# The first two batches of a graph layer put in another order on every engine

## The chip, the cores and the metric

The kernel runs on one core of a Trainium2 chip. The metric is the device time of one execution in microseconds. The core has a matrix engine (TensorE, PE in the rows), VectorE (DVE), ScalarE (ACT), GpSimd (POOL) and SyncE (SP), which here only issues transfers; all five run their own instruction streams and meet at semaphores.

## What is computed

There are 16 graphs (batches) of 512 nodes with 128 features, and a 512x512 adjacency `adj` for each. In the reference both adjacencies `A1` and `A2` are `adj`.

```python
h = jnp.maximum(_layernorm(x, axis=-1), 0.0)
...
eye = jnp.zeros_like(A1) + jnp.eye(N, dtype=A1.dtype)
shifted = jnp.roll(eye, 1, axis=0)
A_fwd = [A1, A2, shifted]
A_list = A_fwd + [jnp.swapaxes(a, 1, 2) for a in A_fwd]
A_list.append(eye)
HW = jnp.einsum('bnf,rfo->rbno', features, W[:, :F]) + jnp.einsum('rd,rdo->ro', W_edges, W[:, F:])[:, None, None, :]
AHW = jnp.einsum('rbnm,rbmo->rbno', A, HW)
out = jnp.max(AHW, axis=0) + b
```

The result is `x + out`. There are seven relations: 0 and 1 with the adjacency, 3 and 4 with its transpose, 2, 5 and 6 with a permutation or identity. A maximum is taken over all seven. Everything is float32.

## The kernel before, in words

The kernel keeps nodes or features on the 128 partitions; `C` = 4 chunks of 128 nodes make a batch. Each float32 operand of a product is split into a rounded part and a rest (`a_hi`, `a_lo`; `at_hi`, `at_lo` for the transposed adjacency; `h_hi`, `h_lo`; `ht_hi`, `ht_lo`; `w_hi`, `w_lo`), and every product is three matmul passes (hi hi, lo hi, hi lo; L697 to L699, in `passes`). ScalarE makes the rounded parts, VectorE and GpSimd subtract to get the rests.

A batch `b = 2k + q` goes through these steps. `x` and four chunks of the adjacency arrive (`x_loaded`, `a_loaded`). VectorE takes mean and variance (`moments`, `mean_and_variance`), a reciprocal root and a shift follow, and ScalarE writes the normalised `h_sb`. TensorE transposes the adjacency (`turn_a`, four transposes for each of four rows of blocks), `h` (`turn_h`) and the row sums (`turn_sums`). Then come `bwd` (four groups of three passes, with `a_hi`, `a_lo`) and `fwd` (four groups, with `at_hi`, `at_lo`), `eye(r)` for relations 2, 5 and 6 (`EYE[0]`, `EYE[1]`, `EYE[2]`) and `along(r)` for the other four, which run one batch later. `join_first` on ScalarE writes `best`, and `join(r)` on VectorE takes the maximum with each further relation, in the order 2, 5, 6, 0, 1, 3, 4. `turn_best` turns the result back, `finish` adds `x` plus bias (`xb_sb`) into `o_sb`, and SyncE stores it.

The row sums take a way of their own: `take_sums` copies them out (`sum_rows`), SyncE writes them to memory and reads them back spread over all partitions (`spread_sums`), and `fill` scales them by `c_col` into the PSUM bank of a relation before `along` accumulates onto it. `c_col` itself, seven columns, comes once from a small matmul of `we_sb` and `wedge_cols`, which VectorE copies out.

Each engine's order is written out by hand: a start of its own for batch 0, `first_step()` (the rest of batch 0 with the beginning of batch 1), `later_batches` (which calls `step` for batch 1, loops over the middle ones and ends with batches 14 and 15), and a last part. The first batch is special: its row-chunks of `h` are rounded singly, and its PSUM banks are others (`rel_bank`, `at_bank`).

SyncE's queue is a single stream: `x` and adjacency of batch 0, `x` of batch 1, small tensors, adjacency of batch 1, `w_sb`, `bias_sb`. After that `reload_x` waits for `h_ready` and `xb_ready` of the buffer's last batch, and `spread_sums` stands behind `reload_a`.

## Time and profile before

| | |
|---|---|
| median of 3 runs | 234.81 us (234.61 to 235.4) |
| the profiled execution | 235.27 us, of which the span is 232.7 us |
| TensorE busy | 221.6 us, 95% of the span |
| ScalarE, VectorE, GpSimd busy | 186.4, 176.4, 143.5 us |
| mean granted clock | 0.977 |

All times in rows count from the span's start. A timeline row gives the start, the duration, the engine, the line of the program, the operation with its output and inputs, how many instructions it merges, and in brackets how long the engine idled before and who ended it. Passes of TensorE overlap: each shows 0.39 us where the next starts 0.23 us later.

### The profile page before, as it was taken

Reading aid. Unit: us, or ns where it says so; the run is one execution under the profiler, and the core shown is the slowest. Engines: PE = TensorE matmul, PEld = TensorE weight load, DVE = VectorE, ACT = ScalarE, POOL = GpSimd, SP = SyncE. Lnnn points to the kernel's source line nnn. Section 1 sums busy time; section 2 is a strip of 40 time slices with the busy share of each in tenths; the row PEclk is TensorE's granted clock in tenths of the full one; section 3 lists DMA queues with packets and bytes.
Section 4 is the critical chain, followed back from the end, with each engine's and each line's share of the span. In section 5 each row is a group of like instructions: output and inputs, shape, how many; then the busy total and the mean of one; then the engine's idle time right before and its main releaser. Section 6 shows DMA issues by size and latency. Waiting matters only on the chain.

```text
span 232.7 us, 4799 instructions
## 1 busy us (share of the span) xinstructions
PE 221.6 (95%) x1133; PEld 183.1 (79%) x1133; DVE 176.4 (76%) x385; ACT 186.4 (80%) x467; POOL 143.5 (62%) x165
## 2 busy tenths in 40 slices
PE   7894899999999999999999999999999999999993
PEld 5483678888888888888888888888888888888772
DVE  3883839788687978778787978878787978858574
ACT  2976569888898988888898988888897988887660
POOL 2427574939668484949669493948669493946400
PEclk9997589999999999999999999999999999999999
DMA  5922565263736445273735535373726535302302
GB/s 197 326 62 57 177 226 171 66 215 130 224 101 197 164 127 185 96 225 118 218 116 177 185 100 186 120 226 107 238 106 175 183 97 182 133 2 103 123 22 69
DMA packets 30385, 34.50 MB, mean 148 GB/s; under 512 B 2104, under 2 KB 20136, under 8 KB 30376
## 3 DMA queue, kind: packets, MB, share of 16 engines
q1 hardware_dynamic: 30375, 34.41, 46.1%
q8 instruction: 3, 0.05, 0.1%
q14 instruction: 7, 0.05, 0.1%
HBM read 30.14 MB, written 4.26 MB: 148 GB/s over the span
## 4 chain that ended last, share of the span: by engine, by line
PE 88%; DVE 4%; DMA 2%; issue 2%; ACT 1%; POOL 1%; SPq 1%; DVEq 0%; ACTq 0%; POOLq 0%
PE at_ps L667 11%; PE rel_ps L697 11%; PE rel_ps L699 11%; PE rel_ps L698 11%; PE fwd_ps L697 6%; PE bwd_ps L697 6%; PE fwd_ps L699 6%; PE fwd_ps L698 6%; PE bwd_ps L699 6%; PE bwd_ps L698 6%; PE turn_ps L679 3%; PE turn_ps L693 3%; DMA a_sb<-in_adj 2%; DVE best L523 1%; DVE w_lo L536 1%
## 5 line engine op out<-in xcount | busy, mean ns | idle before, releaser
L259 POOL TENSOR_TENSOR a_lo<-a_sb,a_hi 128x512 fp32r<-128x512 f32 x60 | 76.4, 1296 | 46.5 <-ACT a_hi L325 46.5
L523 DVE TENSOR_TENSOR best<-rel_ps,best 128x512 f32<-128x512 f32 x62 | 42.4, 685 | 18.0 <-PE rel_ps L699 17.1
L494 DVE TENSOR_TENSOR at_lo<-at_ps,at_hi 128x512 fp32r<-128x512 f32 x62 | 40.9, 683 | 6.4 <-ACT at_hi L333 6.4
L373 ACT ACTIVATE rel_ps<-sum_all,c_col 128x512 f32<-128x512 f32 (+1 forms) x63 | 41.7, 678 | 4.6 <-DVE best L523 2.7
L333 ACT ACTIVATE at_hi<-at_ps 128x512 fp32r<-128x512 f32 x62 | 36.3, 590 | 6.1 <-PE at_ps L667 6.0
L325 ACT ACTIVATE a_hi<-a_sb 128x512 fp32r<-128x512 f32 x64 | 39.4, 616 | 0.2 <-DMA a_sb<-in_adj 0.2
L667 PE MATMUL at_ps<-ident,a_sb 128*128 128x128 f32 x240 | 32.1, 277 | 0.0
L667 PEld LDWEIGHTS at_ps<-ident,a_sb 128*128 128x128 f32 x240 | 28.9, 143 | 4.0
L520 DVE SCALAR_TENSOR_TENSOR best<-rel_ps,c_col,best 128x512 f32<-128x512 f32 x32 | 24.0, 751 | 8.8 <-PE rel_ps L699 7.6
L697 PE MATMUL fwd_ps<-at_hi,h_hi 128*128 128x512 f32 x64 | 27.4, 427 | 1.1 <-issue 1.1
L697 PE MATMUL bwd_ps<-a_hi,h_hi 128*128 128x512 f32 x64 | 26.7, 417 | 0.7 <-issue 0.6
L343 ACT ACTIVATE h_sb<-x_sb,shift,rstd 128x128 f32<-128x128 f32 x60 | 24.6, 483 | 1.7 <-POOL shift L253 1.7
L699 PE MATMUL fwd_ps<-at_hi,h_lo 128*128 128x512 f32 x64 | 25.7, 401 | 0.0
L698 PE MATMUL fwd_ps<-at_lo,h_hi 128*128 128x512 f32 x64 | 25.5, 398 | 0.0
L699 PE MATMUL bwd_ps<-a_hi,h_lo 128*128 128x512 f32 x64 | 25.2, 393 | 0.0
L267 POOL TENSOR_TENSOR h_lo<-h_sb,h_hi 128x512 fp32r<-128x512 f32 x15 | 19.2, 1278 | 9.5 <-DVE h_hi L488 9.5
L698 PE MATMUL bwd_ps<-a_lo,h_hi 128*128 128x512 f32 x64 | 25.0, 390 | 0.0
L381 ACT ACTIVATE best<-rel_ps,c_col 128x512 f32<-128x512 f32 x16 | 11.0, 688 | 14.5 <-PE rel_ps L699 14.5
L697 PE MATMUL rel_ps<-ht_hi,w_hi 128*128 128x512 f32 x48 | 19.8, 412 | 2.9 <-ACT sum_rows L368 2.9
L274 POOL TENSOR_TENSOR xb_sb<-x_sb,bias_sb 128x512 f32<-128x512 f32 x16 | 20.7, 1297 | 1.4 <-DVE o_sb L530 1.4
L698 PE MATMUL rel_ps<-ht_lo,w_hi 128*128 128x512 f32 x48 | 19.4, 405 | 0.0
L699 PE MATMUL rel_ps<-ht_hi,w_lo 128*128 128x512 f32 x48 | 19.4, 403 | 0.0
(103 smaller groups left out, 441.5 us busy)
## 6 DMA issues: line engine op xcount, KB each, us to landing
a_sb<-in_adj SPq DMA_DIRECT2D x64, 256.0 KB, 4.1
sum_all<-sums_dram SPq DMA_DIRECT2D x16, 512.0 KB, 3.6
x_sb<-in_x SPq DMA_DIRECT2D x16, 256.0 KB, 2.9
out<-o_sb SPq DMA_DIRECT2D x15, 256.0 KB, 2.3
w_sb<-in_L_gnn_W SPq DMA_DIRECT2D x1, 448.0 KB, 6.5
bias_sb<-in_L_gnn_b SPq DMA_DIRECT2D x1, 256.0 KB, 6.8
sums_dram<-sum_rows SPq DMA_DIRECT2D x16, 4.0 KB
out<-o_sb SPq DMA_DIRECT2D x2, 128.0 KB, 1.9
```

What stands on the lines that cost most here:

```text
L259: pool.tensor_tensor(a_lo[q][:, j, :], a_sb[q][:, j, :], a_hi[q][:, j, :].bitcast(fp32), ALU.subtract).then_inc(a_lo_ready[j], 1)
L325: act.activation(a_hi[q][:, j, :], a_sb[q][:, j, :], ACT.Copy, accum_out=sums[q][:, 0, j:j + 1]).then_inc(a_hi_ready[j], 1)
L333: act.activation(at_hi[q][:, i, :], at_bank(b, i)[:], ACT.Copy, accum_out=sums[q][:, 1, i:i + 1]).then_inc(at_hi_ready[i], 1)
L343: last = act.activation(h_sb[q][:, j, :], x_sb[q][:, j, :], ACT.Relu, bias=shift[q][:, j:j + 1], scale=rstd[q][:, j:j + 1])
L373: act.activation(to[:, cols], sum_all[q][:, 0 if r in FWD else 1, cols], ACT.Copy, scale=c_col[:, r:r + 1]).then_inc(after_it, 1)
L494: dve.tensor_tensor(at_lo[q][:, i, :], at_bank(b, i)[:], at_hi[q][:, i, :].bitcast(fp32), ALU.subtract).then_inc(at_lo_ready[i], 1)
L520: dve.scalar_tensor_tensor(out=best[q][:], in0=held[:], scalar=c_col[:, r:r + 1], in1=best[q][:], op0=ALU.add, op1=ALU.max).then_inc(joine ...
L523: dve.tensor_tensor(best[q][:], held[:], best[q][:], ALU.max).then_inc(joined[r], 1)
L667: last = pe.transpose(at_bank(b, i)[:, j * P:(j + 1) * P], a_sb[q][:, j, i * P:(i + 1) * P], ident[:])
L697: pe.matmul(out, w_hi_, m_hi, start=start, stop=False, skip_group_check=onto)
L698: pe.matmul(out, w_hi_, m_lo, start=False, stop=False, skip_group_check=onto)
L699: return pe.matmul(out, w_lo_, m_hi, start=False, stop=stop, skip_group_check=onto)
```

## The change

The same instructions run, with two additions on ScalarE's stream: it issues chunks 1 and 3 of the first adjacency itself, and it runs one tiny activation before its first real one, which places the load of its tables ahead of the wait for data. SyncE holds back everything behind the first chunks until chunk 0 has landed. The order of the rest changes on all engines within batches 0 and 1; the buffers of relations 5 and 6 in batch 0 swap; and in the last part `turn_best` and `finish` of batch 14 move behind the first relation of batch 15. The `h_lo` chunks 1 to 3 of batch 0 move from GpSimd to VectorE, and its `a_lo` chunks 2 and 3 from VectorE to GpSimd. The middle of the loop is as before. The diff, cut to its core, with the engine at the head of each piece:

```diff
@@ sync @@
             load_x(0, 0)
+            load_a(0, 0, 0)
+            load_a(0, 0, 2)
+
+            sp.wait_ge(a_loaded[0][0], 16)
+            load_x(0, 1)
+            sp.dma_start(w_sb[:], ...).then_inc(w_loaded, 16)
             for j in range(C):
-                load_a(0, 0, j)
-            load_x(0, 1)
+                load_a(0, 1, j)
             sp.dma_start(we_sb[:], W[:, F:FE, :]).then_inc(we_loaded, 16)
@@ gpsimd @@
             def first_step():
                 ahead = (0, 1)
+                split_a(0, 0, 2)
+                split_a(0, 0, 3)
+                reciprocal_std(*ahead)
                 pool.wait_ge(w_hi_ready, 1)
                 pool.tensor_tensor(w_lo[:, W_DVE:, :], ...)
-                reciprocal_std(*ahead)
                 pool.wait_ge(bias_loaded, 16)
                 add_bias(0, 0)
                 split_h(*ahead)
-                split_a(*ahead, 0)
-                split_a(*ahead, 1)
...
-            for j in range(1, C):
-                chunk, last = h_sb[0][:, j, :], j == C - 1
-                pool.wait_ge(h_hi_ready if last else h0_hi_ready, 1 if last else j + 1)
-                pool.tensor_tensor(h_lo[0][:, j, :], ...)
@@ scalar, first_step @@
                 act.activation(w_hi[:], w_sb[:], ACT.Copy).then_inc(w_hi_ready, 1)
-                round_bwd(0, 0)
-                round_a(*ahead, 0)
                 round_at(*ahead, 0)
                 round_at(*ahead, 1)
                 normalise(*ahead)
+                round_a(*ahead, 0)
                 take_sums(0, 0)
+                round_ht(*ahead)
                 act.wait_ge(c_ready, 1)
                 join_first(0, 0)
                 round_fwd(0, 0)
-                round_a(*ahead, 1)
-                round_ht(*ahead)
-                round_a(*ahead, 2)
-                round_a(*ahead, 3)
@@ scalar, step @@
                 fill(*prev, FWD[1], rel_ps[BANK[FWD[1]]], filled[FWD[1]])
+                if isinstance(b, int) and b == 1:
+                    round_a(k, q, 1)
+                    round_a(k, q, 2)
+                    round_bwd(*prev)
+                    round_a(k, q, 3)
@@ scalar, start @@
-            act.wait_ge(ident_ready, 1)
+            for j in (1, 3):
+                act.dma_start(a_sb[0][:, j, :], ...).then_inc(a_loaded[0][j], 16)
+
+            act.wait_ge(consts_ready, 1)
+            act.activation(neg_mean[1][:], minus_one[:], ACT.Copy)
...
-            for j in range(C - 1):
-                round_a(0, 0, j)
+            round_a(0, 0, 0)
+            round_a(0, 0, 1)
             act.wait_ge(x_loaded[0], 16)
             act.wait_ge(shift_ready, 1)
             for j in range(C):
                 normalise_chunk(j)
-            round_a(0, 0, C - 1)
+            round_a(0, 0, 2)
+            round_a(0, 0, 3)
@@ vector, first_step @@
-                moments(*ahead)
-                dve.wait_ge(bn_done, 2)
-                mean_and_variance(1)
@@ vector, start @@
+            moments(0, 1)
+            dve.wait_ge(bn_done, 2)
+            mean_and_variance(1)
+            for i in range(C):
+                split_at(0, 0, i)
...
-            finish(k, 0)
             split_bwd(k, q)
             join(k, q, FWD[0])
+            finish(k, 0)
@@ tensor @@
             def first_step():
                 ahead = (0, 1)
-                for j in range(C):
-                    bwd(0, 0, j)
+                bwd(0, 0, 0)
+                bwd(0, 0, 1)
                 turn_h(0, 0)
+                bwd(0, 0, 2)
                 fwd(0, 0, 0)
+                bwd(0, 0, 3)
                 fwd(0, 0, 1)
+                fwd(0, 0, 2)
+                turn_a(*ahead, 0)
+                fwd(0, 0, 3)
+                turn_a(*ahead, 1)
                 pe.wait_ge(we_loaded, 16)
                 pe.wait_ge(wedge_cols_ready, 1)
                 pe.matmul(rel_ps[0][:, 0:R], we_sb[:], wedge_cols[:], ...).then_inc(c_multiplied, 1)
                 turn_sums(0, 0)
-                fwd(0, 0, 2)
-                turn_a(*ahead, 0)
-                fwd(0, 0, 3)
-                turn_a(*ahead, 1)
...
                 eye(0, 0, EYE[0])
-                eye(0, 0, EYE[2])
-                pe.wait_ge(sum_rows_ready, 1)
                 eye(0, 0, EYE[1])
                 turn_h(*ahead)
                 turn_a(*ahead, 2)
                 turn_a(*ahead, 3)
+                eye(0, 0, EYE[2])
...
             along(k, q, FWD[0])
+            turn_best(k, 0, B)
             along(k, q, FWD[1])
```

In the tables that follow a row is one instruction in the order of its engine, with the semaphores it waits for. First TensorE near the end of `first_step`: `at_ps` is what `turn_a` of batch 1 writes, `fwd_ps` the product with the transposed adjacency, and the matmul from `wedge_cols` is the one for `c_col`. Before, up to the last row ahead of `eye(0, 0, EYE[0])`:

```order
L770 MATMUL rel_ps<-wedge_cols,we_sb 128x7 [waits wedge_cols_ready,we_loaded]
L686 MATMUL rel_ps<-ident,sums 8x128 [waits at_hi_ready3,a_hi_ready3]
L697 MATMUL fwd_ps<-at_hi,h_hi 128x512 [waits at_lo_ready2,at_hi_ready2]
L698 MATMUL fwd_ps<-at_lo,h_hi 128x512
L699 MATMUL fwd_ps<-at_hi,h_lo 128x512
L667 MATMUL at_ps<-ident,a_sb 128x128 [waits a_loaded1_3,a_loaded1_2,at_lo_ready2,a_loaded1_1,a_loaded1_0]
L667 MATMUL at_ps<-ident,a_sb 128x128 x3
L697 MATMUL fwd_ps<-at_hi,h_hi 128x512 [waits at_lo_ready3,at_hi_ready3]
L698 MATMUL fwd_ps<-at_lo,h_hi 128x512
L699 MATMUL fwd_ps<-at_hi,h_lo 128x512
L667 MATMUL at_ps<-ident,a_sb 128x128 [waits at_lo_ready3]
L667 MATMUL at_ps<-ident,a_sb 128x128 x3
```

After, from the second `turn_a` of batch 1 up to the passes of `eye(0, 0, EYE[0])`:

```order
L671 MATMUL at_ps<-ident,a_sb 128x128 [waits at_lo_ready3]
L671 MATMUL at_ps<-ident,a_sb 128x128 x3
L781 MATMUL rel_ps<-wedge_cols,we_sb 128x7 [waits wedge_cols_ready,we_loaded]
L690 MATMUL rel_ps<-ident,sums 8x128 [waits at_hi_ready3,a_hi_ready3]
L701 MATMUL rel_ps<-ht_hi,w_hi 128x512 [waits ht_hi_ready,c_ready,ht_lo_ready,w_lo_ready,w_hi_ready]
L702 MATMUL rel_ps<-ht_lo,w_hi 128x512
L703 MATMUL rel_ps<-ht_hi,w_lo 128x512
```

The small matmul and the turn of the sums stood ahead of `fwd` 2 and 3 and of both `turn_a`; now they stand behind all of them and directly ahead of `eye`.

VectorE at the same place in the program, from the `ht_lo` of batch 0 on. Before:

```order
L501 TENSOR_TENSOR ht_lo<-turn_ps,ht_hi 128x512 [waits ht_hi_ready]
L629 COPY c_col<-rel_ps 128x7 [waits c_multiplied]
L536 TENSOR_TENSOR w_lo<-w_sb,w_hi 128x384 [waits w_hi_ready]
L475 BN_STATS stats<-x_sb 128x6 [waits x_loaded1]
L475 BN_STATS stats<-x_sb 128x6 x3
L480 BN_AGGR mean_var<-stats 128x2 [waits bn_done]
L480 BN_AGGR mean_var<-stats 128x2 x3
L494 TENSOR_TENSOR at_lo<-at_ps,at_hi 128x512 [waits at_hi_ready0]
L494 TENSOR_TENSOR at_lo<-at_ps,at_hi 128x512 [waits at_hi_ready1]
```

And after:

```order
L508 TENSOR_TENSOR ht_lo<-turn_ps,ht_hi 128x512 [waits ht_hi_ready]
L630 TENSOR_TENSOR wedge_cols<-wedge,own_relation 112x7 [waits wedge_loaded,own_relation_ready]
L633 COPY c_col<-rel_ps 128x7 [waits c_multiplied]
L543 TENSOR_TENSOR w_lo<-w_sb,w_hi 128x384 [waits w_hi_ready]
L501 TENSOR_TENSOR at_lo<-at_ps,at_hi 128x512 [waits at_hi_ready0]
L501 TENSOR_TENSOR at_lo<-at_ps,at_hi 128x512 [waits at_hi_ready1]
```

The moments of batch 1 (BN_STATS, BN_AGGR) have left this place; `w_lo` still stands behind the copy of `c_col`, which waits for the small matmul.

VectorE in the last part, from the last `fwd_lo` on. Before:

```order
L506 TENSOR_TENSOR fwd_lo<-fwd_ps,fwd_hi 128x512 [waits fwd_hi_ready]
L530 TENSOR_TENSOR o_sb<-turn_ps,xb_sb 128x512 [waits out_stored0,xb_ready,best_turned]
L511 TENSOR_TENSOR bwd_lo<-bwd_ps,bwd_hi 128x512 [waits bwd_hi_ready]
L523 TENSOR_TENSOR best<-rel_ps,best 128x512 [waits joined6,rel_done0]
L523 TENSOR_TENSOR best<-rel_ps,best 128x512 [waits joined0,rel_done1]
L523 TENSOR_TENSOR best<-fwd_ps,best 128x512 [waits joined1,rel_done3]
L644 TENSOR_TENSOR best<-rel_ps,best 128x256 [waits half_done,joined3]
```

And after:

```order
L513 TENSOR_TENSOR fwd_lo<-fwd_ps,fwd_hi 128x512 [waits fwd_hi_ready]
L518 TENSOR_TENSOR bwd_lo<-bwd_ps,bwd_hi 128x512 [waits bwd_hi_ready]
L530 TENSOR_TENSOR best<-rel_ps,best 128x512 [waits joined6,rel_done0]
L537 TENSOR_TENSOR o_sb<-turn_ps,xb_sb 128x512 [waits out_stored0,xb_ready,best_turned]
L530 TENSOR_TENSOR best<-rel_ps,best 128x512 [waits joined0,rel_done1]
L530 TENSOR_TENSOR best<-fwd_ps,best 128x512 [waits joined1,rel_done3]
L648 TENSOR_TENSOR best<-rel_ps,best 128x256 [waits half_done,joined3]
```

The `o_sb` of batch 14 moved from ahead of `bwd_lo` to behind the join of relation 0.

## Rows read from the trace of the kernel before

**Rows 1.** The page: the granted clock in 40 slices, in tenths of full speed.
```profile
PEclk9997589999999999999999999999999999999999
```

**Rows 2.** Windows: stretch, its length, busy us per engine, PEclk, DMA share, GB/s.
```profile
4.00:6.00 2.00, 2.00 (x7) 1.30 (x6) 0.97 (x8) 1.72 (x2) 0.81 (x1) 1.00 0.92 323
20.75:21.00 0.25, 0.00 (x0) 0.00 (x0) 0.00 (x0) 0.25 (x2) 0.08 (x1) 0.55 0.00 0
31.00:31.25 0.25, 0.25 (x3) 0.20 (x2) 0.00 (x0) 0.00 (x0) 0.25 (x1) 0.97 0.12 49
36.00:48.00 12.00, 12.00 (x62) 9.96 (x60) 9.94 (x23) 10.83 (x27) 8.45 (x11) 1.00 0.39 124
```

**Rows 3.** Timeline of TensorE, start us, us, engine, operation, [idle before].
```profile
14.59 0.28 PE L770 MATMUL rel_ps<-wedge_cols,we_sb 112*128 112x7 f32 x2
...
17.02 0.48 PE L697 MATMUL rel_ps<-ht_hi,w_hi 128*128 128x512 f32 x1
...
18.26 0.40 PE L699 MATMUL rel_ps<-ht_hi,w_lo 128*128 128x512 f32 x1
21.57 0.79 PE L697 MATMUL rel_ps<-ht_hi,w_hi 128*128 128x512 f32 x1 [2.91 <-ACT sum_rows L368]
...
26.90 0.77 PE L697 MATMUL fwd_ps<-at_hi,h_hi 128*128 128x512 f32 x1 [1.12 <-issue]
...
28.32 0.63 PE L697 MATMUL rel_ps<-ht_hi,w_hi 128*128 128x512 f32 x1
...
29.59 0.63 PE L697 MATMUL fwd_ps<-at_hi,h_hi 128*128 128x512 f32 x1
...
35.51 0.60 PE L679 MATMUL turn_ps<-ident,h_sb 128*128 128x128 f32 x4
```

**Rows 4.** Timeline of ScalarE.
```profile
4.27 1.28 ACT L325 ACT_TABLE_LOAD   x1 [4.27 <-DMA a_sb<-in_adj]
...
7.84 1.65 ACT L440 ACTIVATE h_sb<-x_sb,shift,rstd 128x128 f32<-128x128 f32 x4
...
10.01 0.57 ACT L333 ACTIVATE at_hi<-rel_ps 128x512 fp32r<-128x512 f32 x1
...
31.71 1.30 ACT L373 ACTIVATE rel_ps<-sum_all,c_col 128x512 f32<-128x512 f32 x2 [1.19 <-DMA sum_all<-sums_dram]
```

**Rows 5.** Timeline of VectorE, first two batches.
```profile
3.56 0.87 DVE L475 BATCH_NORM_STATS2 stats<-x_sb 128x6 f32<-128x128 f32 x4 [1.76 <-DMA x_sb<-in_x]
...
4.88 0.16 DVE L592 TENSOR_TENSOR var_eps<-mean_var,eps 128x4 f32<-128x4 f32 x1
...
8.63 0.29 DVE L611 TENSOR_TENSOR h_lo<-h_sb,h_hi 128x128 fp32r<-128x128 f32 x1
...
14.91 0.17 DVE L629 COPY c_col<-rel_ps 128x7 f32<-128x7 f32 x1 [0.19 <-PE rel_ps L770]
14.99 1.63 DVE L536 TENSOR_TENSOR w_lo<-w_sb,w_hi 128x384 fp32r<-128x384 f32 x1
...
25.35 0.74 DVE L520 SCALAR_TENSOR_TENSOR best<-rel_ps,c_col,best 128x512 f32<-128x512 f32 x1
26.01 0.68 DVE L506 TENSOR_TENSOR fwd_lo<-fwd_ps,fwd_hi 128x512 fp32r<-128x512 f32 x1
```

**Rows 6.** Timeline of GpSimd.
```profile
5.19 1.03 POOL L309 TENSOR_TENSOR rstd<-var_eps,minus_half 128x4 f32<-128x4 f32 x1 [3.71 <-DVE var_eps L592]
...
19.57 1.26 POOL L274 TENSOR_TENSOR xb_sb<-x_sb,bias_sb 128x512 f32<-128x512 f32 x1
```

**Rows 7.** Timeline of the SyncE queue's DMA issues.
```profile
20.92 0.37 SPq L173 DMA_DIRECT2D x_sb<-in_x  x1
...
23.31 0.33 SPq L197 DMA_DIRECT2D sums_dram<-sum_rows  x1
```

**Rows 8.** Timeline of VectorE, last microseconds.
```profile
224.79 0.68 DVE L530 TENSOR_TENSOR o_sb<-turn_ps,xb_sb 128x512 f32<-128x512 f32 x1
...
227.58 0.69 DVE L523 TENSOR_TENSOR best<-fwd_ps,best 128x512 f32<-128x512 f32 x1
```

46 lines of the change are left out of this document (21 added, 25 removed).

## The prediction

> **What bounds the kernel now.** I read the page first. TensorE is busy almost throughout, and its granted clock [rows 1] is full except in the slices between about 17 and 35 us. The windows [rows 2] say the rest of the run leaves little to gain: from 36 to 48 us TensorE is busy for all 12.00 us at full clock. So only the first 35 us and the last few can change, and the loop carries whatever is won to the end.
>
> The timeline of TensorE [rows 3] shows two holes there. One is 2.91 us long and ends at 21.57, when ScalarE has copied the row sums. The other, 1.12 us, ends at 26.90; the `fwd_lo` of VectorE finished at 26.01 + 0.68 = 26.69 [rows 5]. During the first hole the granted clock falls from full (2.4 GHz) to half (1.2 GHz): the window 20.75 to 21.00 has mean 0.55. It is back by 31.00 [rows 2], after 4.1 us of unbroken work from 26.90. What it costs stands in the timeline: a group of three passes takes 29.59 - 28.32 = 1.27 us, against some 0.70 at full clock (the six passes from 17.02 to 18.26 + 0.23 take 1.4).
>
> I therefore follow the new order by hand to two marks: the first `fwd` of batch 1 (26.90 before) and the `turn_h` of batch 2 (35.51 before), from where TensorE works without a hole [rows 2, 3].
>
> **Start.** ScalarE lost 1.28 us to its table load after waiting 4.27 us for data [rows 4]; that leaves the path. What then gates is `x`: it landed at 3.56, its variance was ready at 4.88 + 0.16, the power on GpSimd ran 5.19 to 6.22 [rows 5, 6], and `h` could have begun about 3.56 + 2.95 = 6.5 instead of 7.84 [rows 4], since only one `a_lo` instead of two stands ahead of the shift. The other bound is that `x` has to share with chunk 1, which ScalarE issues at the same time: at 323 GB/s [rows 2] 256 KB take 0.81 us. So `h` starts at 6.5 to 7.3. I take the middle, 6.9.
>
> The Trainium skill, "DMA: Bandwidth & Descriptors", section "Issuing engines are not separate DMA queues", speaks against a gain here: transfers issued by several engines run on the same 16 engines and interleave, and only issue time is saved. By it the upper end, 7.3, would hold, and the result would be 0.4 us later; no row of before shows two queues.
>
> **First groups.** After the shift VectorE has the second `a_lo` (to 7.5), four casts with their `h_lo` at about 0.5 each [rows 5] (to 9.5) and the moments of batch 1, by the row of batch 0 some 1.3 (3.56 to 4.88), to 10.8. The first `at_lo` (0.68, as `fwd_lo`) ends at 11.5, later than ScalarE's first `at_hi`, which starts 0.94 earlier with `h` but has one more `a_hi` (0.6) ahead: 10.01 - 0.94 + 0.6 + 0.57 = 10.2 [rows 4]. GpSimd's new `a_lo` for chunks 2 and 3, each 1.26 like its `xb_sb` [rows 6], start when the third `a_hi` is done, near 6.9 + 1.65 + 0.7 = 9.25, and end at 11.8, under the first `fwd`. So TensorE runs from about 11.7: five groups of 0.70 and two `turn_a` of 0.44 (four transposes, the 0.60 of row 35.51 less the 0.16 that the next overlaps) make 4.4, to 16.0. It was 17.02 before with the small matmul already done: 1.0 gained.
>
> **A new wait.** The small matmul moves from 14.59 [rows 3] to 16.0, behind these groups. VectorE's copy of `c_col` waits for it, and `w_lo` is queued behind the copy, 1.63 us [rows 5]. Before, `w_lo` was over at 16.62, hidden by `fwd` 2 and 3 and the turns up to 17.02; that cover is gone. Now: 16.0 + 0.28, copy to 16.4, `w_lo` to 18.05, TensorE at 18.25. So `eye` starts 1.2 us later than before, a hole of nearly 2 us.
>
> **The old hole.** Moments of batch 1 and GpSimd's reciprocal now stand ahead of `w_lo`, so the sum of rows is ready near 19.3 and nobody waits; the 2.91 go. TensorE: two `eye` (1.4) to 19.65, `turn_h` to 20.25 with its tail. Then a chain on two engines, which the two `turn_a` and the third `eye` only partly cover: `ht_hi` 0.5, `best` 0.66, join 0.67, `ht_lo` 0.61, join 0.66, `fwd_lo` 0.68, 0.21 until TensorE starts [rows 5, 3]: 4.0. ScalarE's 128x512 operations take 0.57 in [rows 4]. The first `fwd` of batch 1 starts at 24.3 instead of 26.90: **2.6 gained** so far, with a hole of 2.5 us from about 21.8.
>
> **From there to the second mark.** This hole is nearly as long as the one of 2.91, so I let the clock fall again, and return after the 4.1 us that it took from 26.90. At 1.27 a group the first `eye` of batch 1 is read out at 27.0. ScalarE then has `best` 0.63, two fills 1.25 (row 31.71), three `a_hi` and the `bwd_hi` that moved here, 2.4, and `h` 1.65 [rows 4]: 32.9, and `turn_h` at 33.1. TensorE alone would be there at 32.7. Against 35.51 that is 2.4 gained. The fills need the spread sums. SyncE issues the reload of `x` after `xb_sb`, at 20.92 before [rows 7, 6]; that becomes 16.2 (four `at_hi` from 9.7, `ht_hi` and `w_hi` on ScalarE to about 13.5, an estimate at 0.57 per 512 columns; then two GpSimd operations of about 1.3), and 10.8 us later (31.71 - 20.92) makes 27.0. The store of the sums was issued at 23.31, 2.4 after `x`; it now waits for them until 19.4, 3.2 after. That adds at most 0.8: 27.8, just under the 27.6 to 28.9 of the fills.
>
> **The end.** `o_sb` (0.60 between starts, 224.79) leaves a place where VectorE was waited for by nobody and enters the chain of the last joins. Before, the join at 227.58 waited for TensorE by 0.1 [rows 8]. Now relation 0's join at 225.99 (224.79 + two operations of 0.6), `o_sb` and relation 1's join bring it to 225.99 + 3 x 0.62 = 227.85: 0.27 lost. Bounds are 0 (TensorE or the DMA hides it) and 0.6.
>
> **Sum.** -2.4 + 0.3 = -2.1. Against the profiled execution of 235.27 that is 233.2; its own kernel's median, 234.81, is 0.46 lower, so I forecast 232.8.
>
> **Rivals.** (1) The clock does not fall, since the longest hole is 0.4 us shorter than the old one and work surrounds it. Then ScalarE and the spread sums bound: fills from 27.0, `turn_h` at 27.0 + 1.25 + 2.4 + 1.65 = 32.3, gain 3.2 less 0.3: 231.9. For it: TensorE works right up to 21.8. Against: the old fall came within the hole. (2) The clock falls and stays low as long as before, 10.25 us from 20.75 to 31.00. Then all eight groups up to `turn_h` take 1.27: 24.3 + 10.2 + 0.9 = 35.4, the gain at the mark is 0.1 and the end costs 0.3: 235.0. Against it: after 24.3 no hole like that of 1.12 us interrupts. (3) Slower: the hole ahead of `eye` (2 us, made by `w_lo` behind `c_col`) is enough to lower the clock. Two `eye` and `turn_h` then cost 1.6 more, and if the clock stays low over the eight groups `turn_h` comes at 24.3 + 1.6 + 10.2 + 0.9 = 37.0, 1.5 later: 236.6. It decides only if both hold; with a return after 4.1 us about 1 us of gain remains. (4) The order does what it should, but the two queues delay `x` fully or more: 0.4 less gain, 233.2, and up to 234 if chunk 0 is late as well.
>
> **How the numbers follow.** Forecast 0.44, rival 1 0.27, rival 2 0.09, rival 3 0.08, rival 4 0.12. Differences within 0.3% (0.7 us) are about what a measurement of this kernel can't tell from none. The range runs from rival 1 with 0.5 for the terms under it, 231.3, to 234.3, which holds a low clock of middle length and rival 4, and leaves out rivals 2 and 3. Faster: 0.44 + 0.27 + 0.12 = 0.83; within: 0.09; slower: 0.08.
>
> **What would show it.** The profile after should have: `h` of batch 0 starting near 6.9; `w_lo` of VectorE near 16.4 and the first `eye` waiting for it until about 18.3; no wait for the row sums; the first `fwd` of batch 1 at about 24.3 behind `fwd_lo`; PEclk low for a few microseconds after that; `turn_h` of batch 2 near 33; and at the end the join from `fwd_ps` 0.3 us later relative to TensorE's. I am wrong if `w_lo` is not what `eye` waits for, if the clock behaves otherwise, or if the transfers of two queues delay the start by more than a chunk.

## The result and the profile after

The changed kernel takes 233.18 us (median of 11 runs, 232.42 to 233.52) against 234.81 us (11 runs, 233.77 to 235.62) for the kernel before: a ratio of 0.9927, with a 95% interval of 0.9905 to 0.9949. That is 1.6 to 1.7 us less, inside the predicted range and 0.4 us above the predicted 232.8.

The profiled execution after took 232.42 us (span 229.8), the lowest of its 11, and the one of before 235.27 (span 232.7), above its median. So the two profiles differ by 2.9 us where the medians differ by 1.6. I compare stretches inside the kernel between profiles, and take what a whole kernel gains or loses from the medians.

The granted clock of the page, in 40 slices, and then windows of the changed kernel (columns as in rows 2):

```profile
PEclk9999799999999999999999999999999999999999
```

```profile
24.00:26.00 2.00, 2.00 (x8) 1.63 (x7) 1.55 (x6) 0.69 (x1) 1.39 (x4) 0.72 0.66 250
26.00:28.00 2.00, 2.00 (x6) 1.51 (x6) 0.00 (x0) 1.62 (x3) 1.41 (x2) 0.50 0.01 4
28.00:30.00 2.00, 2.00 (x10) 1.61 (x9) 0.55 (x1) 2.00 (x8) 1.60 (x2) 0.92 0.03 8
```

The clock still falls, but later: it is full up to 24.86, where TensorE had worked for 1.5 us again after its longest hole, is at half (1.2 GHz) until 28.2, and full from then on. Before, it was low from 20.75 to 31.00 [rows 2].

TensorE's timeline of the changed kernel (start, duration, operation, idle time before it and who ended it):

```profile
16.11 0.29 PE L781 MATMUL rel_ps<-wedge_cols,we_sb 112*128 112x7 f32 x2
...
17.17 0.47 PE L701 MATMUL rel_ps<-ht_hi,w_hi 128*128 128x512 f32 x1 [0.64 <-DVE w_lo L543]
...
18.64 0.61 PE L683 MATMUL turn_ps<-ident,h_sb 128*128 128x128 f32 x4
...
23.40 0.47 PE L701 MATMUL fwd_ps<-at_hi,h_hi 128*128 128x512 f32 x1 [2.58 <-issue]
...
24.86 0.59 PE L701 MATMUL fwd_ps<-at_hi,h_hi 128*128 128x512 f32 x1
...
31.63 0.66 PE L683 MATMUL turn_ps<-ident,h_sb 128*128 128x128 f32 x4
...
38.85 0.47 PE L701 MATMUL fwd_ps<-at_hi,h_hi 128*128 128x512 f32 x1 [0.27 <-issue]
...
45.34 0.60 PE L683 MATMUL turn_ps<-ident,h_sb 128*128 128x128 f32 x4
```

The two holes of [rows 3], 2.91 and 1.12 us, are gone; from 17 us to the second `turn_h` of these rows there are three others, of 0.64, 2.58 and 0.27. The first `fwd` of batch 1 starts at 23.40 instead of 26.90, the `turn_h` of batch 2 at 31.63 instead of 35.51. A group of three passes takes 0.70 up to 24.86 (three starts 0.23 apart) and then 1.27.

ScalarE, VectorE, GpSimd and SyncE's queue at the places the prediction named:

```profile
1.79 1.28 ACT L443 ACT_TABLE_LOAD   x1 [1.79 <-issue]
...
7.25 1.65 ACT L446 ACTIVATE h_sb<-x_sb,shift,rstd 128x128 f32<-128x128 f32 x4 [0.44 <-DVE shift L616]
...
26.38 1.30 ACT L373 ACTIVATE rel_ps<-sum_all,c_col 128x512 f32<-128x512 f32 x2 [0.63 <-DMA sum_all<-sums_dram]
...
29.93 1.64 ACT L343 ACTIVATE h_sb<-x_sb,shift,rstd 128x128 f32<-128x128 f32 x4
```

```profile
4.29 0.87 DVE L482 BATCH_NORM_STATS2 stats<-x_sb 128x6 f32<-128x128 f32 x4 [2.50 <-DMA x_sb<-in_x]
...
16.52 0.55 DVE L543 TENSOR_TENSOR w_lo<-w_sb,w_hi 128x384 fp32r<-128x384 f32 x1
```

```profile
13.82 1.28 POOL L284 TENSOR_TENSOR w_lo<-w_sb,w_hi 128x512 fp32r<-128x512 f32 x1
```

```profile
23.00 0.33 SPq L199 DMA_DIRECT2D sum_all<-sums_dram  x1
```

The table load is off the path. `w_lo` on VectorE takes 0.55 us, where it took 1.63 before [rows 5]. The fills start at 26.38, when the spread sums (issued at 23.00) have landed, and `h` of batch 2 follows them and three `a_hi` and a `bwd_hi`: it starts at 29.93, and `turn_h` starts right behind it.

The tail on VectorE, from the join of relation 6 in batch 15 to the one from `fwd_ps` (of [rows 8]):

```profile
220.22 0.75 DVE L527 SCALAR_TENSOR_TENSOR best<-rel_ps,c_col,best 128x512 f32<-128x512 f32 x1 [0.70 <-PE rel_ps L703]
...
222.69 0.69 DVE L530 TENSOR_TENSOR best<-rel_ps,best 128x512 f32<-128x512 f32 x1 [0.47 <-PE rel_ps L703]
223.30 0.68 DVE L537 TENSOR_TENSOR o_sb<-turn_ps,xb_sb 128x512 f32<-128x512 f32 x1
...
224.68 0.69 DVE L530 TENSOR_TENSOR best<-fwd_ps,best 128x512 f32<-128x512 f32 x1
```

From 220.22 to 224.68 are 4.46 us. The first join waits 0.47 us for TensorE, and `o_sb` then stands between two joins.

### The profile page after: what moved, and what is told of

It is laid out like the page before. It is cut to its first block, busy times and chain, and to the rows that moved or that the text cites. A ratio compares the mean times of both kernels' runs of the same rounds, so it can differ in the third digit from the quotient of the medians.

```text
span 229.8 us, 4799 instructions
## 1 busy us (share of the span) xinstructions
PE 217.9 (95%) x1133; PEld 180.6 (79%) x1133; DVE 175.3 (76%) x386; ACT 185.9 (81%) x468; POOL 143.9 (63%) x164
## 4 chain that ended last, share of the span: by engine, by line
PE 89%; DVE 3%; issue 3%; DMA 2%; ACT 1%; POOL 1%; DVEq 0%; ACTq 0%; POOLq 0%
PE at_ps L671 11%; PE rel_ps L701 11%; PE rel_ps L703 11%; PE rel_ps L702 11%; PE fwd_ps L701 7%; PE fwd_ps L702 6%; PE fwd_ps L703 6%; PE bwd_ps L701 6%; PE bwd_ps L703 6%; PE bwd_ps L702 6%; PE turn_ps L683 3%; PE turn_ps L697 3%; DMA x_sb<-in_x 2%; ACT h_sb L446 1%; PE rel_ps L690 1%
## 5 line engine op out<-in xcount | busy, mean ns | idle before, releaser
L261 POOL TENSOR_TENSOR a_lo<-a_sb,a_hi 128x512 fp32r<-128x512 f32 x62 | 79.1, 1297 | 48.3 <-ACT a_hi L325 48.3
L671 PE MATMUL at_ps<-ident,a_sb 128*128 128x128 f32 x240 | 31.2, 272 | 0.0
L671 PEld LDWEIGHTS at_ps<-ident,a_sb 128*128 128x128 f32 x240 | 28.1, 140 | 4.0
```

The lines of the kernel that those rows point to most:

```text
L261: pool.tensor_tensor(a_lo[q][:, j, :], a_sb[q][:, j, :], a_hi[q][:, j, :].bitcast(fp32), ALU.subtract).then_inc(a_lo_ready[j], 1)
L671: last = pe.transpose(at_bank(b, i)[:, j * P:(j + 1) * P], a_sb[q][:, j, i * P:(i + 1) * P], ident[:])
```

## The experiments

All times are medians. The kernels were timed in three groups, each beside the kernel before on one chip: after_again to w_lo_together (before: 234.98), moments_alone to short_chain (234.59), and a_hi_early to moments_sums_first (235.33). Within a group medians can be compared, across groups the ratios to before. The third column is the start of batch 2's `turn_h` in the profile.

| kernel | us (lowest to highest, runs) | `turn_h` | ratio to before (95%) |
|---|---|---|---|
| after_again | 232.83 (231.92 to 233.22, 7) | 32.08 | 0.9907 (0.9871 to 0.9944) |
| tail_old | 232.29 (231.61 to 232.40, 6) | 31.73 | 0.9891 (0.9859 to 0.9924) |
| hole_filled | 232.01 (231.47 to 232.49, 6) | 31.30 | 0.9889 (0.9857 to 0.9921) |
| w_lo_together | 235.33 (235.00 to 235.83, 12) | 35.15 | 1.0017 (0.9996 to 1.0038) |
| moments_alone | 231.88 (231.29 to 232.47, 6) | 31.94 | 0.9878 (0.9850 to 0.9905) |
| transfers_alone | 238.88 (237.75 to 240.47, 6) | 40.79 | 1.0170 (1.0133 to 1.0208) |
| one_queue | 232.97 (231.81 to 234.86, 8) | 31.22 | 0.9939 (0.9908 to 0.9970) |
| short_chain | 232.01 (231.56 to 233.19, 6) | 32.22 | 0.9888 (0.9857 to 0.9919) |
| a_hi_early | 231.77 (231.44 to 232.06, 6) | 30.84 | 0.9842 (0.9812 to 0.9872) |
| wedge_early | 235.04 (234.44 to 236.52, 12) | 35.21 | 0.9983 (0.9954 to 1.0011) |
| short_chain_sums_first | 232.48 (231.27 to 234.14, 6) | 30.64 | 0.9887 (0.9845 to 0.9929) |
| moments_sums_first | 231.86 (230.49 to 232.41, 6) | 32.37 | 0.9835 (0.9797 to 0.9873) |

### The changed kernel once more, and its tail put back

`after_again` is the changed kernel unaltered.

> The changed kernel again, as the measure for the three beside it. Its profiled execution (232.42 us) was the fastest of its eleven, the one of before (235.27 us) among the slower of its own, so the two spans differ by 2.9 us and the medians by 1.6. If that spread is chance, this profile has a span between 229.8 and 231.1 with the same stages: eye of batch 0 near 17.2, the first fwd of batch 1 near 23.4, turn_h of batch 2 between 31.6 and 32.5. If the order had a second state, turn_h would come in two clearly separate places, about 1 us apart.

```profile
23.47 0.48 PE L701 MATMUL fwd_ps<-at_hi,h_hi 128*128 128x512 f32 x1 [2.57 <-issue]
...
32.08 0.66 PE L683 MATMUL turn_ps<-ident,h_sb 128*128 128x128 f32 x4 [1.28 <-ACT h_sb L343]
...
39.43 0.47 PE L701 MATMUL fwd_ps<-at_hi,h_hi 128*128 128x512 f32 x1 [0.42 <-issue]
```

This execution had a mean clock of 1.00: after the same hole of 2.57 us the clock did not fall. Yet `turn_h` comes at 32.08, later than the 31.63 of the profile in which it fell, because it waits 1.28 us for ScalarE's `h_sb`. Over its 7 runs those at 0.99 took 232.68 and 232.91, those at 1.00 between 231.92 and 233.22. So no cost of the clock shows in this kernel. The span, 230.3 us, lies in the expected range; the 229.8 of the first profile was a low one.

`tail_old` puts only the last part back as it was:

```diff
@@ vector @@
+            finish(k, 0)
             split_bwd(k, q)
             join(k, q, FWD[0])
-            finish(k, 0)
             join(k, q, FWD[1])
@@ tensor @@
+            turn_best(k, 0, B)
             along(k, q, FWD[0])
-            turn_best(k, 0, B)
             along(k, q, FWD[1])
```

> The changed kernel with the last part as before: turn_best and finish of batch 14 ahead of the first relation of batch 15. Theory A (mine): o_sb in the chain of the last joins costs time, so from the join of relation 6 (220.22 in the profile after) to the join from fwd_ps it is 4.05 us as before and not 4.46, and the time falls by 0.3 to 0.4 us against the changed kernel. Theory B: the new place hides it, since TensorE no longer turns before it waits for fwd_lo; then the time is the same or up to 0.3 us more.

```profile
220.54 0.75 DVE L527 SCALAR_TENSOR_TENSOR best<-rel_ps,c_col,best 128x512 f32<-128x512 f32 x1 [0.70 <-PE rel_ps L703]
...
224.61 0.69 DVE L530 TENSOR_TENSOR best<-fwd_ps,best 128x512 f32<-128x512 f32 x1
```

The same stretch takes 4.07 us instead of 4.46. The median is 0.54 us lower than that of `after_again`, but the two intervals overlap, so the size rests on the trace: the new tail costs 0.4 us. TensorE's rows show by which way, first in the profile of the changed kernel, then in `tail_old`:

```profile
221.71 0.47 PE L701 MATMUL rel_ps<-fwd_hi,w_hi 128*128 128x512 f32 x1 [0.85 <-DVE fwd_lo L513]
...
222.49 0.60 PE L697 MATMUL turn_ps<-ident,best 128*128 128x128 f32 x4
```

```profile
221.03 0.60 PE L697 MATMUL turn_ps<-ident,best 128*128 128x128 f32 x4
222.04 0.47 PE L701 MATMUL rel_ps<-fwd_hi,w_hi 128*128 128x512 f32 x1 [0.41 <-DVE fwd_lo L513]
```

In both, relation 0 starts on TensorE 1.5 us behind the join of relation 6, when `fwd_lo` is ready. The old tail turned `best` during that wait. The new one waits 0.85 us with nothing to do and turns `best` afterwards, so relation 1 starts 2.63 us behind the join of relation 6 (222.85) instead of 2.28 (222.82 in `tail_old`), and the join from `fwd_ps` waits for TensorE. The `o_sb` between the joins, on which my Theory A put the loss, would by itself have brought VectorE to 224.5 and not 224.68, a loss of 0.2. No run moves one of the two without the other.

### The hole behind `turn_h` of batch 1 filled

Eleven matmuls of zeros into a PSUM bank that is free there stand behind the third `eye`, so that TensorE has work up to the first `fwd` of batch 1.

```diff
@@ tensor, first_step @@
                 eye(0, 0, EYE[2])
+                pe.wait_ge(joined[EYE[0]], 1)
+                for _ in range(11):
+                    pe.matmul(rel_ps[0][:], warm[:, 0:P], warm[:], start=True, stop=True)
```

> The changed kernel with eleven matmuls of zeros (128x512, 0.23 us each at full clock) on TensorE between the third eye of batch 0 and the first fwd of batch 1, into a bank that is free there; nothing else is changed. They fill most of the 2.58 us hole. Theory A: the clock falls because of this hole; with it filled the granted clock stays at full, and passes after 24.9 take 0.23 instead of 0.43 us. But turn_h of batch 2 hangs on ScalarE, whose fills wait for the spread sums (26.38 us), so it stays at 31.6 and the total at the changed kernel's within 0.3 us. Theory B: the half clock is what is left of the loss; then turn_h comes 1 us or more earlier and the total falls by as much. Theory C: the clock falls whatever fills the hole.

```profile
31.30 0.66 PE L683 MATMUL turn_ps<-ident,h_sb 128*128 128x128 f32 x4 [1.28 <-ACT h_sb L343]
```

With the hole filled the clock did not fall, but it had not fallen in `after_again` either. `turn_h` waits for `h_sb` for the same 1.28 us. It comes 0.78 earlier than in `after_again`, and so do the fills (26.05 against 26.84); the first `fwd` of batch 1 is only 0.14 earlier. The 0.8 us lie in the store of the row sums: from its issue to the issue of the load behind it pass 3.00 us here (19.27 to 22.27) and 3.77 in `after_again` (19.41 to 23.18). The same instructions took 3.67 in the first profile of the changed kernel, 3.45 in `tail_old` and 3.15 in `one_queue`. The median is 0.8 lower than that of `after_again`, with overlapping intervals; whether the filling has a part in it isn't told apart by this run. The clock has none that the profile shows.

### `w_lo` of GpSimd and of VectorE at the same time

GpSimd's share of `w_lo` (the first 512 columns) waits until `c_col` is copied, so that both engines start it together, as before the change.

```diff
@@ gpsimd, first_step @@
                 pool.wait_ge(w_hi_ready, 1)
+                pool.wait_ge(c_ready, 1)
                 pool.tensor_tensor(w_lo[:, W_DVE:, :], ...)
```

> The changed kernel with one more wait on GpSimd: its half of w_lo (1.28 us) waits for c_ready too, so it starts together with VectorE's half, as it did in the kernel before; the bias addition behind it moves along. Theory A: VectorE's w_lo took 1.63 us before and 0.55 after because GpSimd's ran beside it before and not after, both reading SBUF. Then it takes about 1.6 again here, or GpSimd's own is stretched instead, and eye starts at 17.9 to 18.3 instead of 17.17. Theory B: the difference comes from something else (the first use after the transfer of w, the PE or DMA traffic at 15 us); then VectorE's stays at 0.55, and eye starts at about 17.95, when GpSimd's half is done. The bias addition ends near 19.2 instead of 16.3, so the reload of x and the spread sums come up to 2 to 3 us later, and the total rises by 1 to 3 us against the changed kernel in either theory.

```profile
16.64 0.55 DVE L544 TENSOR_TENSOR w_lo<-w_sb,w_hi 128x384 fp32r<-128x384 f32 x1
```

```profile
16.87 1.45 POOL L285 TENSOR_TENSOR w_lo<-w_sb,w_hi 128x512 fp32r<-128x512 f32 x1 [2.94 <-DVE c_col L634]
```

```profile
18.42 0.47 PE L702 MATMUL rel_ps<-ht_hi,w_hi 128*128 128x512 f32 x1 [1.77 <-POOL w_lo L285]
...
30.65 0.80 PE L702 MATMUL rel_ps<-fwd_hi,w_hi 128*128 128x512 f32 x1 [2.29 <-ACT rel_ps L374]
```

Now VectorE started first and kept its 0.55 us, and GpSimd's took 1.45 instead of 1.28. That is 0.17 more, where 0.32 us of VectorE's were left when it started, so this run alone separates the two theories by little; `moments_alone` below does it better. `eye` starts at 18.42, near the 18.25 of the prediction, but it waits for GpSimd's part. GpSimd's `w_lo` is 3.05 us later than in the changed kernel; the reload of `x`, queued behind `xb_sb`, moves by 3.2 to 19.66 and the spread sums by 3.3 to 26.28, and TensorE waits 2.29 us for the fill. The median is 2.5 us above `after_again`: the whole gain of the change is lost. At `eye` 1.25 us of it are lost; the fills, at 29.90 after a wait of 2.92 us for the sums, are 3.5 us later than in the first profile of the changed kernel, and `turn_h` as much (35.15).

### One part of the change alone: the moments and the reciprocal

The kernel before, with nothing but this: `moments(0, 1)` and `mean_and_variance(1)` move ahead of the first `split_at` on VectorE, and `reciprocal_std(*ahead)` ahead of `w_lo` on GpSimd.

```diff
@@ vector, start @@
             split_a(3)
+            moments(0, 1)
+            dve.wait_ge(bn_done, 2)
+            mean_and_variance(1)
             split_at(0, 0, 0)
@@ vector, first_step @@
-                moments(*ahead)
-                dve.wait_ge(bn_done, 2)
-                mean_and_variance(1)
                 split_at(*ahead, 0)
@@ gpsimd, first_step @@
                 ahead = (0, 1)
+                reciprocal_std(*ahead)
                 pool.wait_ge(w_hi_ready, 1)
                 pool.tensor_tensor(w_lo[:, W_DVE:, :], ...)
-                reciprocal_std(*ahead)
```

> The kernel before with one part of the change: the moments of batch 1 on VectorE move ahead of the first at_lo of batch 0, and GpSimd's reciprocal of batch 1 ahead of its w_lo. Theory A: the 2.91 us hole hangs on this chain (w_lo, moments, reciprocal, normalise, row sums). Normalise of batch 1 then starts when ScalarE is free, near 17.9 instead of 19.71, TensorE's wait for the row sums ends near 19.9 to 20.3 instead of 21.57, although the first at_lo come 1.2 us later and push TensorE to about 18 for the first eye; the total falls by 1 to 2 us. Theory B: the hole's wait is replaced by another of its size (at_lo later, so fwd and eye later by the whole 1.2), and the total falls by less than 0.5 us.

```profile
19.61 0.50 PE L697 MATMUL rel_ps<-ht_hi,w_hi 128*128 128x512 f32 x1 [1.07 <-ACT sum_rows L368]
...
23.89 0.47 PE L697 MATMUL fwd_ps<-at_hi,h_hi 128*128 128x512 f32 x1 [2.01 <-issue]
...
31.94 0.60 PE L679 MATMUL turn_ps<-ident,h_sb 128*128 128x128 f32 x4
...
45.08 0.60 PE L679 MATMUL turn_ps<-ident,h_sb 128*128 128x128 f32 x4
```

```profile
15.04 0.56 DVE L536 TENSOR_TENSOR w_lo<-w_sb,w_hi 128x384 fp32r<-128x384 f32 x1
```

```profile
15.08 1.67 POOL L280 TENSOR_TENSOR w_lo<-w_sb,w_hi 128x512 fp32r<-128x512 f32 x1 [1.32 <-ACT w_hi L387]
```

The hole of 2.91 us shrinks to 1.07, no slice of the page but the last has a clock below 9, and the ratio to before, 0.9878, is lower than that of the whole change (0.9907 and 0.9927). Its `turn_h` of batch 2 comes at 31.94, 0.3 later than in the profile of the changed kernel, but the next one at 45.08 against 45.34: the changed kernel loses 0.6 us between the two (13.71 against 13.14 us), nearly all of it ahead of the first `fwd` of batch 2, and then its 0.4 in the tail. So one short move gives all of the gain that was measured. The rest of the change sums to a loss, by the ratios of 0.7 us against `after_again` and of 1.2 against the first measurement; the intervals overlap with the one and just touch with the other, so that there is a loss rests on the two places in the trace.

This run also settles what `w_lo` costs. VectorE's starts at 15.04, where it started at 14.99 before [rows 5], with the same transfers around it, and takes 0.56 us instead of 1.63. What differs is that GpSimd's now starts 0.04 us behind it and not ahead, and the delay is on GpSimd's side.

### The transfers alone, and the small load

`transfers_alone` is the kernel before with the new transfers: two chunks on ScalarE's queue, the rest held back until chunk 0 has landed, the early table load.

```diff
@@ sync @@
             load_x(0, 0)
-            for j in range(C):
-                load_a(0, 0, j)
+            load_a(0, 0, 0)
+            load_a(0, 0, 2)
+
+            sp.wait_ge(a_loaded[0][0], 16)
             load_x(0, 1)
+            sp.dma_start(w_sb[:], ...).then_inc(w_loaded, 16)
+            for j in range(C):
+                load_a(0, 1, j)
             sp.dma_start(we_sb[:], W[:, F:FE, :]).then_inc(we_loaded, 16)
...
-            for j in range(C):
-                load_a(0, 1, j)
-            sp.dma_start(w_sb[:], ...).then_inc(w_loaded, 16)
@@ scalar, start @@
-            act.wait_ge(ident_ready, 1)
+            for j in (1, 3):
+                act.dma_start(a_sb[0][:, j, :], ...).then_inc(a_loaded[0][j], 16)
+
+            act.wait_ge(consts_ready, 1)
+            act.activation(neg_mean[1][:], minus_one[:], ACT.Copy)
```

> The kernel before with another part of the change alone: chunks 1 and 3 of the first adjacency from ScalarE's queue, everything behind the first chunks held until chunk 0 has landed, and the table load ahead of the data. The compute order is that of before. Theory A: the head gains little by it: x lands at 4.29 instead of 3.56 and chunk 0 at about 5.45 instead of 4.27, which takes back most of the 1.28 us of the table load; ScalarE's first at_hi starts between 9.7 and 10.1 (10.01 before), the hole for the row sums stays near 2.9, and the total moves by less than 0.7 us. Theory B: the transfers are a main part of the gain; then the total falls by 1 us or more.

```profile
15.62 0.17 DVE L626 TENSOR_TENSOR wedge_cols<-wedge,own_relation 112x7 f32<-112x7 f32 x1 [4.43 <-DMA wedge<-in_L_gnn_W_edges]
```

```profile
16.54 0.76 PE L703 MATMUL bwd_ps<-a_hi,h_hi 128*128 128x512 f32 x1 [3.82 <-DVE a_lo L602]
```

This was a miss of mine: 4.3 us slower. `wedge` is now issued behind all large loads, and the old order of VectorE has `wedge_cols` ahead of `a_lo` of the later chunks: it waits 4.43 us for a few hundred bytes, and TensorE 3.82 us for the `a_lo` behind it. `wedge_early` issues `we_sb` and `wedge` directly behind the wait for chunk 0, and changes nothing else of it.

```diff
@@ sync @@
             sp.wait_ge(a_loaded[0][0], 16)
+            sp.dma_start(we_sb[:], W[:, F:FE, :]).then_inc(we_loaded, 16)
+            sp.dma_start(wedge[:], ...).then_inc(wedge_loaded, 16)
             load_x(0, 1)
...
                 load_a(0, 1, j)
-            sp.dma_start(we_sb[:], W[:, F:FE, :]).then_inc(we_loaded, 16)
-            sp.dma_start(wedge[:], ...).then_inc(wedge_loaded, 16)
```

> The kernel before with the change's transfers alone (238.88 us), but with the small loads of the edge weights first behind the held chunk instead of second last. Theory A: of the 4.3 us that the transfers alone cost, most is VectorE waiting 4.43 us for these few hundred bytes, ahead of its a_lo; with them early the wait goes and the total comes to 235.0 to 236.2 us, of which 0.5 to 1 stays for x and chunks that land later. Theory B: the second queue and the hold are the cause; then the total stays above 237.

It took 235.04, the time of the kernel before (0.9983, interval 0.9954 to 1.0011). So the late `wedge` was the whole loss, and the new transfers with the early table load are worth nothing by themselves. In the changed kernel `wedge_cols` stands behind the first `at_lo` and the `ht_lo` of batch 0, starts at 14.37 and waits only 0.50.

`one_queue` is the changed kernel with all four chunks on SyncE's queue:

```diff
@@ sync @@
-            load_a(0, 0, 0)
-            load_a(0, 0, 2)
+            for j in range(C):
+                load_a(0, 0, j)
@@ scalar, start @@
-            for j in (1, 3):
-                act.dma_start(a_sb[0][:, j, :], ...).then_inc(a_loaded[0][j], 16)
```

> The changed kernel with all four chunks of the first adjacency issued by SyncE in their order again; the hold behind them and the early table load stay. Theory A: x no longer shares with chunk 1 and lands near 3.6 instead of 4.29, so h of batch 0 starts near 6.6 instead of 7.25, if chunk 0 also lands near 4.3; the two a_hi are done by then. TensorE's first bwd starts up to 0.6 us earlier, and the total is lower by 0 to 0.5 us than the changed kernel's: the second queue costs a little. Theory B: the second queue saves its issue time; then chunks 2 and 3 land later by 0.5 us or more, the a_hi of chunks 2 and 3 wait for them, and the total rises by 0.3 to 0.6.

`x` landed at 3.63 instead of 4.29 and `h` started at 6.92 instead of 7.25, so the second queue did delay the start, by 0.3 us in these two profiles. The total, 232.97 (231.81 to 234.86), is too spread to tell a difference of that size from none.

### Moving work out of the way of the second mark

`short_chain` is the changed kernel with the old tail, `round_fwd` and `split_fwd` of batch 0 ahead of `round_ht`, `split_ht` and the joins (so that `fwd` of batch 1 can start without the hole), and `bwd_hi` and the `a_hi` of batch 1 ahead of the fills. TensorE gets a wait for the first join of batch 0 ahead of its next use of that bank.

```diff
@@ scalar, first_step @@
+                round_fwd(0, 0)
                 round_a(*ahead, 0)
                 take_sums(0, 0)
                 round_ht(*ahead)
                 act.wait_ge(c_ready, 1)
                 join_first(0, 0)
-                round_fwd(0, 0)
@@ scalar, step @@
                 round_at(k, q, 3)
+                if isinstance(b, int) and b == 1:
+                    round_bwd(*prev)
+                    for j in range(1, C):
+                        round_a(k, q, j)
...
                 fill(*prev, FWD[1], ...)
-                if isinstance(b, int) and b == 1:
-                    round_a(k, q, 1)
-                    round_a(k, q, 2)
-                    round_bwd(*prev)
-                    round_a(k, q, 3)
@@ vector, first_step @@
+                split_fwd(0, 0)
+                split_ht(*ahead)
                 join(0, 0, EYE[1])
-                split_ht(*ahead)
                 join(0, 0, EYE[2])
-                split_fwd(0, 0)
```

> A version meant to beat both: the changed kernel with the last part as before; fwd_hi and fwd_lo of batch 0 ahead of the ht and the joins on ScalarE and VectorE, so that the first fwd of batch 1 need not wait for them (only the first eye does, and it gets a wait for joined of relation 2, which the bank needs); and bwd_hi with the a_hi of chunks 1 to 3 of batch 1 ahead of the fills, where ScalarE stood idle for 2.96 us. Theory A: the first fwd of batch 1 starts near 20.9 instead of 23.40, no hole over 1 us is left until the first along, which waits for the spread sums (27.1), and turn_h of batch 2 comes at 30.3 to 30.8 instead of 31.6; with 0.4 from the end the total is 1.0 to 1.6 us below the changed kernel's. Theory B: the spread sums bound everything behind them, the fills start at 26.4 as now and turn_h stays near 31.4; the gain is then the 0.4 of the end.

```profile
24.74 0.47 PE L700 MATMUL fwd_ps<-at_hi,h_hi 128*128 128x512 f32 x1 [0.88 <-DVE at_lo L500]
...
27.58 0.50 PE L700 MATMUL rel_ps<-fwd_hi,w_hi 128*128 128x512 f32 x1 [1.92 <-ACT rel_ps L373]
```

```profile
26.83 1.30 ACT L373 ACTIVATE rel_ps<-sum_all,c_col 128x512 f32<-128x512 f32 x2 [1.70 <-DMA sum_all<-sums_dram]
```

The first `fwd` came at 20.93, and the hole is only put off: 0.88 and 1.92 us now, the latter until the fill, which itself waits 1.70 us for the spread sums. 2.5 us won at the first mark were worth nothing at the second, so the chain over two engines was not the bound: Theory B. The ratio, 0.9888, is that of `tail_old` (0.9891), whose tail this kernel has. Behind these holes the clock fell after all, at about 28 us, and TensorE reached `turn_h` at 32.22 without waiting.

`a_hi_early` is the changed kernel with the `a_hi` 1 to 3 and the `bwd_hi` ahead of the fills alone (the piece "scalar, step" above and nothing else).

> The changed kernel with one thing taken back to an earlier place: in the step of batch 1 ScalarE makes bwd_hi and the a_hi of chunks 1 to 3 ahead of join_first and the fills, where it stood idle for 2.96 us, instead of behind them. Theory A: what the change gave away behind the second mark hangs on these four: bwd_lo on VectorE waited 3.9 us for bwd_hi, VectorE's chain came late, and the first fwd of batch 2 waited for fwd_lo 0.3 to 0.4 us. Then h of batch 2 follows the fills at once (27.6 instead of 29.9), turn_h is bound by TensorE itself (31.3 to 31.6), the wait ahead of the first fwd of batch 2 is gone, and the total falls by 0.4 to 1.0 us against the changed kernel (232.83 to 233.18). Theory B: the loss behind the mark comes from the later reloads of batch 3, which move little here; then the total falls by less than 0.2 us.

```profile
27.04 1.30 ACT L373 ACTIVATE rel_ps<-sum_all,c_col 128x512 f32<-128x512 f32 x2 [1.20 <-DMA sum_all<-sums_dram]
28.28 1.64 ACT L343 ACTIVATE h_sb<-x_sb,shift,rstd 128x128 f32<-128x128 f32 x4
```

```profile
30.84 0.60 PE L682 MATMUL turn_ps<-ident,h_sb 128*128 128x128 f32 x4
...
38.41 0.47 PE L700 MATMUL fwd_ps<-at_hi,h_hi 128*128 128x512 f32 x1 [0.69 <-issue]
```

```profile
29.95 1.57 DVE L494 CAST h_hi<-h_sb 128x512 fp32r<-128x512 f32 x1 [0.48 <-ACT h_sb L343]
...
33.43 0.87 DVE L481 BATCH_NORM_STATS2 stats<-x_sb 128x6 f32<-128x128 f32 x4 [0.71 <-DMA x_sb<-in_x]
...
37.52 0.68 DVE L512 TENSOR_TENSOR fwd_lo<-fwd_ps,fwd_hi 128x512 fp32r<-128x512 f32 x1
```

The four operations now run while ScalarE waits for the sums; what is left of the wait is 1.20 us, and `h` follows the fills at 28.28 instead of 30.40 (`after_again`). `turn_h` is 1.24 us earlier, the total 1.1 us below `after_again` (1.5 by the ratios), or 1.3% to 1.9% below the kernel before. Its ratio is also below that of `moments_alone`, but there the intervals overlap.

But I had expected the wait ahead of the first `fwd` of batch 2 to vanish, and it grew to 0.69. From the end of `h_sb` (28.28 + 1.64 = 29.92) to the end of `fwd_lo` (37.52 + 0.68 = 38.20) VectorE needs 8.28 us, in `moments_alone` 7.19 (31.01 to 38.20). Two rows differ: the rounding of `h` takes 1.57 us instead of 0.43, beside GpSimd's `a_lo` that started at 29.94, and VectorE stands idle for 0.71 us until `x` of batch 3 lands. Both lead to a part of the change that the expectation left out. GpSimd now has the first two `a_lo` of batch 1 ahead of its `xb_sb`, which ends at 30.00 instead of 27.92 in `moments_alone`, and the reload of `x`, which waits for `xb_sb`, goes out at 30.07 instead of 27.99. This is read from the traces; no run puts these two back.

The last two kernels store the row sums ahead of the reload of `x` and load them back ahead of the reload of the adjacency, since the fills of both versions waited for them. `short_chain_sums_first` is `short_chain` with this edit, `moments_sums_first` is `moments_alone` with it:

```diff
@@ sync @@
-            step(0, 0, True, stored=False)
+            sp.wait_ge(sum_rows_ready, 1)
+            sp.dma_start(sums_dram[0][:, :], sum_rows[0][:]).then_inc(sums_stored[0], 16)
+            reload_x(0, 0)
+            sp.wait_ge(sums_stored[0], 16)
+            sp.dma_start(sum_all[0][:]..., sums_dram[0]...).then_inc(sums_spread[0], 16)
+            reload_a(0, 0)
```

> The version short_chain (232.01 us) with SyncE's stream changed for batch 0: the store of the row sums and the load of the spread sums go out ahead of the reload of the adjacency, which they followed until now (the reload of x goes between the two). Theory A: the fills waited 1.70 us for the spread sums behind 1.3 MB of reloads; now the store is issued near 20.1, lands near 22 instead of 23.4, and the spread sums land near 25.2 instead of 26.8. The first along starts near 25.7 instead of 27.58, turn_h of batch 2 comes near 29.8 to 30.3 instead of 32.2, and the total is 1.5 to 2.3 us lower, 229.7 to 230.5. Theory B: the reload of the adjacency of batch 2, 4 us later than now, becomes the next wait (turn_a at 29 us or the a_hi behind it), and the gain is under 0.5 us.

```profile
26.84 1.30 ACT L380 ACTIVATE rel_ps<-sum_all,c_col 128x512 f32<-128x512 f32 x2 [1.89 <-DVE best L533]
```

The sums are spread more than 1 us sooner, and the fill starts at the same 26.84: it now waits for a join of VectorE. Expected was a gain of 1.5 to 2.3 us, measured none (0.9887 against 0.9888); a second engine stood right behind the first. The runs fall into two groups, three of 231.3 to 231.8 at a clock of 0.991 to 0.997 and three of 233.2 to 234.1 at 0.985, so here the clock seems to cost. The two profiles bear it out: the fills start at 26.84 here and at 26.83 in `short_chain`, and the matmul behind them at 27.58 in both, but `turn_h` comes at 30.64 with the clock full and at 32.22 with the clock fallen, 1.6 us later.

> The kernel before with the moments and the reciprocal of batch 1 moved (moments_alone, 231.88 us) and with the spread of the first sums ahead of the reload of the adjacency in SyncE's stream. Theory A: fills at 28.13 waited 1.86 us for the spread sums; the store goes out near 19.5 instead of 20.48 and no longer behind the reloads, so they land near 25 and the fills follow best at 26.2. The first along starts near 26.7 to 27.1 instead of 28.87, and the total falls by 1.2 to 2.0 us to about 230.2. Theory B: as with short_chain, the late reload takes the place of the wait, and the gain is under 0.5 us.

```profile
24.31 0.76 PE L704 MATMUL fwd_ps<-at_hi,h_hi 128*128 128x512 f32 x1 [2.01 <-issue]
```

```profile
26.00:28.00 2.00, 2.00 (x6) 1.55 (x6) 1.06 (x2) 0.77 (x2) 1.92 (x3) 0.57 0.81 312
```

On top of `moments_alone` the same edit removes the wait of the fills as well. The profiled execution shows what takes its place: the clock fell right at 24.31, after a hole of 2.01 us, and stayed at half until about 27.7, and `turn_h` came at 32.37. Two runs of 6 had a clock of 1.00 and took 230.49 and 230.85; the other four, at 0.985 to 0.992, took 231.67 to 232.41. So in this kernel the clock seems to cost about 1.4 us, by two runs against four. By the ratios the edit gains 1.0 us on `moments_alone`, between the two theories, and the intervals overlap.

## Why the prediction was right in sign and off in its parts

**The mechanism held.** The 2.91 us for the row sums went because the moments and the reciprocal stand ahead of `w_lo`; `moments_alone` shows that this move by itself brings all of the gain that the whole change brings.

**The start.** `x` landed at 4.29 and `h` began at 7.25, at the upper end of 6.5 to 7.3, not in the middle. The small matmul came at 16.11 (16.0 forecast). The Trainium skill, "DMA: Bandwidth & Descriptors", section "Issuing engines are not separate DMA queues", was right on this term: `one_queue` got `x` at 3.63.

**The term that was most wrong is `w_lo`: 1.63 us read as its cost.** It takes 0.55. Before, GpSimd's part of `w_lo`, which stands in no row shown so far, was running when VectorE's started:

```profile
14.91 1.29 POOL L279 TENSOR_TENSOR w_lo<-w_sb,w_hi 128x512 fp32r<-128x512 f32 x1 [3.30 <-ACT w_hi L387]
```

It ended at 16.20; VectorE's instruction, from 14.99, ended at 16.62 [rows 5], 0.42 us behind it (a little under its own 0.55; ends on GpSimd are rough). In the changed kernel GpSimd's ran from 13.82 to 15.10, alone, and VectorE's took 0.55. In `moments_alone` VectorE's started 0.04 us ahead and took 0.56, and GpSimd's was stretched to 1.67. `w_lo_together` has the same order and a stretch of 0.17. The one that starts second takes longer by nearly what is left of the other's: 1.08 us where 1.21 were left before, 0.39 where 0.52 were left, 0.17 where 0.32 were. So 1.1 of the 1.63 us was waiting.
The Trainium skill, "SBUF — State Buffer", section "Who interferes with whom", states it: a VectorE instruction with two inputs in SBUF contends with a GpSimd instruction that reads SBUF, and order of issue decides who blocks. The trace agrees, with the 0.55, 1.63 and 1.67 above. I did not apply it; it would have put the first `eye` at 17.2 instead of 18.25.

From there on my steps were 1 to 1.5 us late: first `fwd` of batch 1 at 23.40 (24.3), `turn_h` of batch 2 at 31.63 or 32.08 (33.1). The chain from `turn_h` to `fwd`, forecast at 4.0 us with a hole of 2.5, took 4.15 (23.40 less 18.64 + 0.61) with a hole of 2.58.

**The fills.** I had them at 27.6; they started at 26.38 (26.84 in `after_again`). The first `eye` of batch 1 was read out at 25.06 instead of 27.0, as it began 0.9 us earlier and ran at full clock. What the fills then waited for were the spread sums, and these came earlier than my 27.8 too: their load was issued 3.67 us behind their store, against 4.56 before. My working also called 27.8 "just under" 27.6 to 28.9, which it is not; by it the forecast should have been 0.2 us later.

**The clock.** It fell in the profiled execution and not in another; the forecast counted a fall in every one. It cost nothing that shows, since ScalarE and the spread sums bound the second mark (`h_sb` ended at 31.57, `turn_h` started at 31.63), as rival 1 had it. So rival 1 had the bound right, and its `turn_h` at 32.3 lies nearer than my 33.1; the forecast had the fall right. Rival 3 fell: the hole ahead of `eye` is 0.64 us and the clock is full behind it. Rival 2 fell with the clock's return after 3.4 us. Rival 4 had the late `x` right; that its 233.2 is the measured time is chance, since `w_lo` and the tail were priced in it as in the forecast.

**What the prediction did not see.** First, the wait ahead of the first `fwd` of batch 2. It starts 0.87 us behind `turn_best` (38.85, 37.98) where it was 0.35 before (42.14, 41.79), which is nearly all of the 0.56 us by which the stretch from one `turn_h` to the next has grown (13.71 against 13.15). The matmul waits for `fwd_lo`. VectorE needs 7.1 us from the end of `h_sb` to the end of `fwd_lo` (31.57 to 38.64), no more than before (34.59 to 41.78); but before, `h_sb` was ready 0.92 us ahead of `turn_h`, and now 0.06. The three `a_hi` and the `bwd_hi` that moved behind the fills have taken this lead. They did it through `h`, and not through `bwd_lo` and the joins behind it, as I had put it in the expectation of `a_hi_early`: VectorE had those done 0.21 us before `h_sb` came. In `a_hi_early`, where the four run earlier, the lead is 0.92 again, and by the traces it is GpSimd's order that makes the chain longer there. I had written that from the second mark on TensorE works without a hole, which was read from before and not worked out for after. Second, the tail: 0.27 us forecast by way of `o_sb` on VectorE, 0.4 measured by way of `turn_best` on TensorE, which the prediction did not follow there.

**The sum.** Between the two profiles: 3.9 us won at `turn_h`, 0.6 lost up to the next one, 0.4 lost in the tail, 2.9 in all, which is the difference of the spans. Forecast were 2.4 won, 0.3 lost (235.27 less 2.1 less 0.46 is 232.7, not 232.8). The medians say 1.6; the profile of before lies 0.46 above its median and that of after 0.76 below, which is the other 1.2 or so. So the closeness of 232.8 to 233.18 is partly luck: an underestimated gain stood against two losses that were missed or too small.

**What stays open.** Why the clock falls in one execution and not in the next at the same hole; what it would bring to put GpSimd's `a_lo` of batch 1 back behind `xb_sb`; and how much of the 0.8 us between `hole_filled` and `after_again` is the filling and how much the spread in the landing of the row sums.

## What to carry to other kernels

Read a VectorE duration beside GpSimd's timeline before using it as a cost: where the same shape is shorter elsewhere, the difference is waiting, and it vanishes or moves to GpSimd with the order of the two. In a reorder of everything, try its parts alone: here one move of moments and a reciprocal gave 1.2%, and the rest took some 0.3 to 0.5% of it back. Where two engines work through a stretch side by side, follow both: the tail lost its time on TensorE, where only VectorE had been worked out. And where an engine keeps its pace but a wait appears, look for a lead that is gone. After a hole is closed, follow the next reader of the same data (fills, spread sums, join, clock) one by one, since here each stood within 1 us of the one before it.

## What the runs showed that I had not expected

- The rounding of `h` to `h_hi` on VectorE, 128x512, has one input and still depends on GpSimd: 0.43 us at 18.57 in the profile of the changed kernel, where GpSimd idled, 0.87 us in the same profile beside GpSimd's `a_lo`, 1.57 us in `a_hi_early` (the row at 29.95), and 1.16 us in `w_lo_together` beside GpSimd's `xb_sb`. It is 0.43 us again before the change and in `moments_alone`, where GpSimd idled.
- A load of a few hundred bytes that is issued last, behind the large ones, held up VectorE for 4.43 us and the kernel for 3.8 us (238.88 against 235.04 with it issued early; 4.4 us by the ratios).
- A hole of 2.57 or 2.58 us ahead of the same matmul was followed by a fall to half clock in one execution (1.5 us later) and by none in another; ahead of it TensorE had been busy but for holes under 1 us in both.
